# The last expert layer's sixteen indirect writes of kept blocks: at most two in flight

## The reference, cut to what matters

```python
logits = x @ gate_w.T
routing_weights, selected = phi_routing(logits)          # two experts for each row
wte = zeros((T, E)).at[arange(T)[:, None], selected].add(routing_weights)
for e in range(E):
    h = silu(x @ w1[e].T) * (x @ w3[e].T)
    out = out + wte[:, e:e + 1] * (h @ w2[e].T)
```

## Time and profile before

| | us |
|---|---|
| timed runs, median of 3 | 1807.62 |
| timed runs, lowest and highest | 1802.72, 1809.69 |
| span of the profiled execution (first to last instruction) | 1839.1 |
| PE busy in the span | 1491.7 (81%) |
| POOL busy in the span | 943.4 (51%) |
| mean granted TensorE clock | 0.897 |

### The profile page before, as it was taken

How to read it: one execution, slowest core, us unless ns; L and a number is a source line. 1 busy time by engine, 2 the same in 40 slices (tenths; PEclk the granted TensorE clock), 3 DMA queues, 4 the chain that set the end, 5 groups by cost and what they waited for, 6 DMA issues and landing times. The chain is left out here.

```text
span 1839.1 us, 29734 instructions
## 1 busy us (share of the span) xinstructions
PE 1491.7 (81%) x10638; PEld 1231.6 (67%) x10638; DVE 1062.8 (58%) x2174; ACT 901.8 (49%) x1610; POOL 943.4 (51%) x742
## 2 busy tenths in 40 slices
PE   5887888899968768944299997985885999899984
PEld 2566666678746668923168887972774788788873
DVE  6777879689768653456744554457746323233223
ACT  5897797999645534624132234534442322232221
POOL 0599798899738627810011236020624429582771
PEclk8899999899988969976589999988886999899987
DMA  3001010101030075340000000030043503242144
GB/s 130 24 25 47 24 44 28 47 38 55 1 107 2 2 243 181 118 142 17 2 0 1 1 1 1 1 88 7 1 159 142 142 3 116 81 144 75 52 139 163
DMA packets 54577, 119.21 MB, mean 65 GB/s; under 512 B 14448, under 2 KB 35443, under 8 KB 46884
## 3 DMA queue, kind: packets, MB, share of 16 engines
q1 hardware_dynamic: 45556, 84.38, 13.3%
q0 software_dynamic: 8448, 32.91, 5.5%
q10 hardware_dynamic: 432, 0.03, 0.0%
HBM read 92.78 MB, written 24.43 MB: 64 GB/s over the span
## 5 line engine op out<-in xcount | busy, mean ns | idle before, releaser
L878 POOL TENSOR_TENSOR HC<-H,CB 128x512 f32<-128x512 f32 x256 | 321.7, 1287 | 77.1 <-DVE H L786 63.2
L604 ACT ACTIVATE UT<-DTXT,BT 128x512 f32<-128x512 f32 x256 | 181.5, 711 | 28.2 <-PE ps L452 27.8
L452 PE MATMUL ps<-ident,UT 128*128 128x128 f32 x1024 | 166.8, 289 | 28.5 <-DVE H L786 16.6
L452 PEld LDWEIGHTS ps<-ident,UT 128*128 128x128 f32 x1024 | 124.3, 147 | 89.7 <-DVE H L786 40.6
L614 ACT ACTIVATE dA<-DT,nA 128x512 f32<-128x512 f32 x256 | 181.3, 710 | 3.4 <-DVE H L786 3.3
L786 DVE TENSOR_TENSOR_SCAN H<-dA,ps 128x512 f32<-128x512 f32 x128 | 152.3, 1212 | 45.1 <-PE ps L452 36.8
L786 DVE TENSOR_TENSOR_SCAN H<-dA,HL,ps 128x512 f32<-128x512 f32 x128 | 157.5, 1269 | 25.7 <-PE ps L452 17.6
L461 PE MATMUL ps<-ident,HC 128*128 128x128 f32 x1024 | 158.1, 282 | 11.2 <-POOL HC L878 9.2
L2317 DVE TENSOR_TENSOR f_XN<-f_XN,ps 128x1024 f32<-128x1024 f32 x39 | 47.6, 1222 | 178.1 <-PE ps L160 150.2
L158 PE MATMUL ps<-f_W,f_DIT 128*128 x312 | 130.1, 417 | 10.3 <-POOL f_W L2023 7.1
L461 PEld LDWEIGHTS ps<-ident,HC 128*128 128x128 f32 x1024 | 123.0, 146 | 19.1 <-POOL HC L878 18.7
(11 more groups left out here) (558 smaller groups left out, 4159.0 us busy)
## 6 DMA issues: line engine op xcount, KB each, us to landing
CB<-m_c_rows SPq DMA_DIRECT2D x16, 1024.0 KB
f_w<-in_f_w SPq DMA_DIRECT2D x16, 1024.0 KB, 5.2
f_stage<-in_f_w POOLq DMA_DIRECT2D x15, 1024.0 KB, 5.2
f_stage<-in_f_w SPq DMA_DIRECT2D x9, 1024.0 KB, 4.9
f_xn_rows<-f_XN SPq DMA_DIRECT2D x8, 512.0 KB, 12.0
f_W<-f_y_rows SPq DMA_DIRECT2D x4, 1024.0 KB, 9.2
f_rows_in<-f_DI SPq DMA_DIRECT2D x23, 128.0 KB
f_DI<-f_rows_in SPq DMA_DIRECT2D x23, 128.0 KB, 2.3
```

Source lines behind the costliest of these rows:

```text
L452: ins = pe.transpose(PS[4 + G % UR][:, t * P:(t + 1) * P], UT[:, n % 2, t, c * P:(c + 1) * P], g.ident[:, :])
L604: act.activation(UT[:, N % 2, t, :], DTXT[:, k % 2, t, :], ACT.Copy, scale=BT[:, k % 2, t, n:n + 1]).then_inc(ut_ready, 1)
L878: pool.tensor_tensor(HC[:, y, :], H[:, s, :], CB[:, n // 4 % CR, n % 4, :], ALU.mult).then_inc(hc_ready, 1)
```

## The change

The sixteen writes of kept blocks count in two new semaphores, `kept_out`, in turn. From the third on, each write waits until the last but one has landed, so that at most two are in flight. The first fetch waits for both semaphores to be full in place of `scattered`, and SP's wait for `scattered` counts sixteen writes fewer.

```diff
--- before.py
+++ after.py
@@ -1931,6 +1931,7 @@
         h1_ready, h3_ready, sg_ready, hh_ready = sem("h1_ready"), sem("h3_ready"), sem("sg_ready"), sem("hh_ready")
         htp_ready, ht_ready, eo_ready, eo_copied = sem("htp_ready"), sem("ht_ready"), sem("eo_ready"), sem("eo_copied")
         stored = [sem(f"stored{i}") for i in range(2)]
+        kept_out = [sem(f"kept_out{i}") for i in range(2)]
         gathered = [sem(f"gathered{i}") for i in range(NT // 4)]
         hi_ready, lo_ready, ditl_ready, htl_ready = sem("hi_ready"), sem("lo_ready"), sem("ditl_ready"), sem("htl_ready")
         added, room_free, out_stored = sem("added"), sem("room_free"), sem("out_stored")
@@ -1979,7 +1980,7 @@
                         sp.dma_start(rows_out[o * P:(o + 1) * P, :], EO[:, o % 2, :]).then_inc(stored[o % 2], 16)
                 for free in slot_free:
                     sp.wait_ge(free, 16)
-                sp.wait_ge(scattered, 16 * (MB - len(slot_free)))
+                sp.wait_ge(scattered, 16 * (MB - KEPT - len(slot_free)))
                 for j in range(NT // 4):
                     sp.dma_start(GR[:, 4 * j:4 * j + 4, :, :],
                                  y_rows[1 + 8 * j * P:1 + 8 * (j + 1) * P, :].rearrange("(t p q) d -> p t q d", p=P, q=2)).then_inc(
@@ -2048,14 +2049,17 @@
 
                 def fetch_back(n):
                     if n == 0:
-                        pool.wait_ge(scattered, 16 * KEPT)
+                        for out in kept_out:
+                            pool.wait_ge(out, 16 * (KEPT // 2))
                     if n >= KEPT:
                         pool.wait_ge(slot_free[n - KEPT], 16)
                     pool.wait_ge(stored[n % 2], 16 * (n // 2 + 1))
                     pool.dma_start(kept[:, n % KEPT, :], rows_out[(KEPT + n) * P:(KEPT + n + 1) * P, :]).then_inc(fetched[n % 4], 16)
                 for k in range(KEPT):
                     pool.wait_ge(eo_copied, k + 1)
-                    scatter(k, kept[:, k, :], scattered)
+                    if k >= 2:
+                        pool.wait_ge(kept_out[k % 2], 16 * (k // 2))
+                    scatter(k, kept[:, k, :], kept_out[k % 2])
                 last = MB - 2 - KEPT
                 for i in range(last + 2):
                     if i < last:
```

## The result

| us | before | after |
|---|---|---|
| timed runs, median | 1808.44 (12 runs) | 1813.35 (12 runs) |
| lowest and highest | 1802.72, 1813.06 | 1810.73, 1816.5 |
| span of the profiled execution | 1839.1 | 1811.7 |
| its time | not recorded | 1813.47 |

What follows compares the result with a forecast made beforehand. The kernel was taken as bound by a mostly-PE chain. Timed 1807.6 us, plus 0.6 (3.7 us more on POOL less 3.1 covered), minus 0 for a stall held absent from timed runs, gave 1808.2 us; range 1795 to 1813.

Steps and rivals of the forecast that it cites:

- What the change does to the rhythm: POOL's sixteen writes: two, briefly three, are already in flight; a POOL that waits wakes late, so writes start in pairs.
- The price of a pair: POOL's bounded writes: pairs start 3.12 us apart instead of 2.59, 7 x 0.53 = 3.7 us more on POOL.
- My near bound: Upper limit for a pair of POOL's writes: 2.48 us to land and wake SP plus 0.90 us, 3.38 us.
- my far one: Farther upper limit for a pair: an indirect gather's 3.3 us to landing plus 0.90, 4.2 us; 11.3 us on POOL.
- The cover: POOL's idle time behind the writes, 17.8 us less PE's 14.7 us, hides 3.1 us of the delay, leaving +0.6 us.
- The stall: PE's loss beside the sixteen writes in the profile: expected to shrink there, but held absent from timed runs, gaining 0.
- the 14.7 us: PE's excess over three blocks at 9.5 us each, from 1726.73 to 1769.96 in the first profile, beside POOL's writes.
- My count of 28.0 us of losses: PE losses beside indirect DMA bursts, 14.7, 7.4 and at most 5.9 us: nearly all of the 31.5 us span difference.
- My threshold between 1.43 and 1.58 us: Spacing of POOL's gathers: PE lost time at 1.43 us and not at 1.58; bounded writes would be 1.56 apart.
- The stall is real and goes: Rival: engines truly wait during POOL's 1.29 us writes and the wider rhythm ends it: 1793.5 us, chance 0.17.
- The lanes don't overlap and POOL becomes the end: Rival: paired writes land one behind the other, 6.24 us a pair, burst 25.6 us longer: 1830 us, chance 0.05.
- The change does nothing: Rival: two in flight already, POOL's waits met on arrival: 1807.6 us; counted within the forecast's 0.78.

Runs made afterwards that it cites:

- the POOL delay: The kernel before, writes unbounded, with two POOL operations on a buffer no longer read put in front of the sixteen writes: 1812.24 us, ratio 1.0026.

## Why the prediction was right or wrong

**What the change does to the rhythm: right in kind.** It hardly lowers the number in flight but makes POOL wake late, writes come in pairs, and nothing else in the kernel pays. The profile after shows exactly that, and eight in flight shows that the waits as such are free.

**The price of a pair: this term failed.** I took 3.12 us for each of seven pairs, 3.7 us in all. The five plain pairs took 3.29 us on average, and two took 5.16 and 4.99 us: 5 x 0.70 + 2 x 2.49 = 8.5 us over the old 2.59. Of the 4.8 us that I missed, 1.2 are the plain price (a write and a write, where I took a fetch and a write), and 3.6 are the two pairs beside instruction fetches, which I had no term for at all. With the plain price alone my sum would have read 7 x 0.70 - 3.1 = +1.8, 1809.4 us, well inside the range: the missing term is the step that failed. My near bound, 3.38 us, was right for a plain pair; my far one, 4.2 us, was exceeded by the two. The range was also cut short: the median plus the far bound is 1807.6 + 8.2 = 1815.8 us, and I took the scatter of the runs off that, though scatter widens a range and doesn't narrow it. A median over undisturbed landings can't bound what a waiting engine pays, since it pays each late one in full.

**The cover: nearly right.** I took 17.8 - 14.7 = 3.1 us from a disturbed execution; it is 2.7 us, and with one in flight the same 2.7 us come out. From first write to last POOL needs 72.93 - 64.13 = 8.8 us more, and 8.8 - 2.7 = 6.1 us come out at the end in the trace; the timed interval is 3.1 to 6.5 us. With 8.8 and 3.1 my own sum would have read +5.7, 1813.3 us.

**The stall: the conclusion held, its reasons did not.** That the 14.7 us are not in the timed runs was right, and the gain they promised did not exist. (My count of 28.0 us of losses held 2.5 us at the gathers that belong to the start of the stage; about 8 us, not 5.9, were lost in the first expert layer, where the same instruction of ACT starts at 706.22 us in the first profile and at 698.11 in the second.) But I thought that the rhythm of 1.29 us brought the stall about, that 1.56 us might end it, and that an execution choking on its records was the likely cause. The second profile of before, eight in flight and the POOL delay all write at 1.29 us under the same profiler and show nothing. What happened in that one execution stays open: no later profile has it. With this the page of the Trainium skill that I cited on the pushing back of event records is neither borne out nor refuted; no run here shows it. My threshold between 1.43 and 1.58 us was read from the same disturbed execution and means nothing.

**The rivals.** "The stall is real and goes" fell with the second profile. "The lanes don't overlap and POOL becomes the end" had the right end with the wrong mechanism: the lanes do overlap (the second of a pair costs 1.3 us), yet POOL ends the kernel. I had let this happen only from 4.3 us a pair, for a loss of half a per cent; a loss at all begins at 2.59 + 2.7 / 7 = 3.0 us, and the mean pair took 3.8 (two pairs were over my 4.3, five under it). "The change does nothing" is refuted by the interval.

## What to carry to other kernels

Before bounding what an engine has in flight, ask what that engine does behind it and how many microseconds it has to spare before someone waits for it; here 2.7 us decided. An engine that waits for each DMA pays landing and waking, and every late landing in full; with one more in flight (three, not two) the bound was free here. And compare the span of a profiled execution with the timed runs before explaining anything in it: 31.5 us too many meant that the most conspicuous stall of the page was in no timed run.

## What the runs showed of the hardware that was not expected

A 128 KB indirect write from SBUF lands 2.4 to 2.5 us after its start. Where one 16 KB packet of PE's instruction fetch starts 0.3 to 2.6 us after it, it mostly lands after 2.8 to 4.5 us, since one of its sixteen increments is late (4.34 us where the other fifteen were there by 2.56). Other traffic makes all sixteen late: by up to 0.5 us beside SP's store and load of 128 KB each, and by 2.8 us behind a 1 MB load of POOL's own. From the landing to the start of the next indirect write of a waiting POOL another 0.8 us pass (3.24 us from write to write), where back-to-back writes are 1.29 us apart.

And one execution of an unchanged kernel ran 1839.1 us with PE held up beside indirect DMAs, where the second profile of the same kernel has a span of 1809.6 us and those of the changed ones 1805.5 to 1814.5 us (1838.1 with one in flight).
